# A first stage without loops, mask transposes between its node tiles, small loads from ScalarE's queue, and features stored unscaled

## The reference

```
h   = relu(layernorm(x))
g   = (h * node_weights + node_bias + h) @ W
h0  = layernorm(g) * gamma + beta                # features; also the residual
s1  = h0 @ a1;  s2 = h0 @ a2
att = softmax(where(adj > 0, leaky_relu(s1_i + s2_j), -9e15))
x   = x + elu(att @ h0 + h0)
```

## Time and profile before

| | |
|---|---|
| median of 3 runs | 3704.32 us (3702.21 to 3707.39) |
| profiled execution, time | 3706.8 us |
| its span, first to last instruction | 3705.0 us |
| busy, share of the span | TensorE 93%, VectorE 84%, ScalarE 47%, GpSimd 48% |
| mean granted TensorE clock | 0.965 |
| span of first stage and barrier | up to 203.8 us |
| attention stage of layer 0, first matmul | 212.57 us |
| adding up of its last half ends | about 679.5 us |

### The profile page before, as it was taken

The page is one execution under the profiler, slowest core; times in us unless marked ns, Lnnn a source line. Parts: engine busy times, 40 slices in busy tenths (PEclk is TensorE's granted clock), DMA queues, the critical chain, the costliest instruction groups (busy, mean ns, idle before and its releaser), DMA issues. The chain is left out here.

```text
span 3705.0 us, 59650 instructions
## 1 busy us (share of the span) xinstructions
PE 3456.8 (93%) x21147; PEld 1823.0 (49%) x21147; DVE 3098.7 (84%) x7016; ACT 1736.4 (47%) x3578; POOL 1778.2 (48%) x832
## 2 busy tenths in 40 slices
PE   5679999678999999999999999999997999699999
PEld 4579999542111111111111111111116999699999
DVE  6878888577999999999999999999956776477777
ACT  7821111355666666666666666666662444300100
POOL 2400000113888888888888888888890111000000
PEclk8789999888999999999999999999997999899999
DMA  6522121473001110010001111011003332211220
GB/s 237 199 98 87 52 86 58 149 252 116 24 11 28 28 28 15 19 30 28 28 5 28 28 28 28 7 28 28 5 5 104 115 115 81 115 47 61 84 83 27
DMA packets 80079, 240.72 MB, mean 65 GB/s; under 512 B 13616, under 2 KB 40624, under 8 KB 65584
## 3 DMA queue, kind: packets, MB, share of 16 engines
q1 hardware_dynamic: 79792, 236.92, 18.9%
HBM read 151.80 MB, written 85.07 MB: 64 GB/s over the span
## 5 line engine op out<-in xcount | busy, mean ns | idle before, releaser
L1472 POOL TENSOR_TENSOR a_w<-a_w,keep_mask_t 128x1024 f32<-128x1024 f32 x768 | 1627.4, 2145 | 301.1 <-ACT a_w L1457 301.1
L1457 ACT ACTIVATE a_w<-a_sc_ps 128x512 f32<-128x512 f32 x2048 | 1111.4, 595 | 718.1 <-PE a_sc_ps L1379 716.4
L1412 DVE CUSTOM_DVE_ANT_0 a_mx_ps<-a_mx_ps,a_mbias 128x512 f32<-128x512 f32 x1992 | 1310.5, 718 | 74.0 <-PE a_mx_ps L1341 73.2
L1357 PE MATMUL a_o_ps<-a_w,a_v 128*33 128x512 f32 x4096 | 1081.0, 606 | 6.0 <-POOL a_w L1472 5.8
L868 PE MATMUL g_acc<-g_hv,g_w 128*128 128x129 f32 x8192 | 923.6, 276 | 43.2 <-ACT g_hv L825 32.3
L868 PEld LDWEIGHTS g_acc<-g_hv,g_w 128*128 128x128 f32 x8192 | 922.1, 193 | 44.9 <-DVE g_w L804 44.9
L804 DVE SCALAR_TENSOR_TENSOR g_w<-g_row,keep_s,keep_mask_t 128x1024 f32<-128x1024 f32 x512 | 647.1, 1282 | 201.9 <-PE g_acc L868 185.0
L1379 PE MATMUL a_sc_ps<-a_qs,a_ks 97*128 97x512 f16 x2048 | 621.9, 385 | 0.3
L1425 DVE TENSOR_TENSOR a_w<-a_w,keep_mask_t 128x1024 f32<-128x1024 f32 x256 | 457.7, 1788 | 34.0 <-ACT a_w L1457 28.6
L1341 PEld LDWEIGHTS a_mx_ps<-a_ks,a_qs 32*128 32x128 f16 x1992 | 88.9, 91 | 789.3 <-DVE a_mx L1412 427.9
L1341 PE MATMUL a_mx_ps<-a_ks,a_qs 32*128 32x512 f16 x1992 | 376.6, 385 | 7.5 <-DVEq L1429 7.5
(11 more groups left out here) (237 smaller groups left out, 2237.5 us busy)
## 6 DMA issues: line engine op xcount, KB each, us to landing
h_nodes<-p_h SPq DMA_DIRECT2D x16, 1032.0 KB, 3.9
g_h<-h_nodes SPq DMA_DIRECT2D x16, 1032.0 KB, 7.4
p_adj_in<-in_adj SPq DMA_DIRECT2D x16, 1024.0 KB, 8.3
g_row<-u_rows SPq DMA_DIRECT2D x32, 512.0 KB, 7.3
v<-p_v SPq DMA_DIRECT2D x32, 264.0 KB, 3.0
a_v<-v SPq DMA_DIRECT2D x16, 528.0 KB, 3.6
p_x<-in_x SPq DMA_DIRECT2D x8, 1024.0 KB, 5.0
mask_bias<-p_mbias SPq DMA_DIRECT2D x16, 512.0 KB, 8.9
```

What stands on the lines that cost most here:

```text
L1357: mm = nc.tensor.matmul(o_ps[2 * HD * a:2 * HD * a + HD + 1, c % 2, :], v[u][:, jt, a, :], w[:, g % PB, a, :], start=(jt == 0), stop=(jt = ...
L1412: last = nc.vector.tensor_tensor_reduce(out=mx_ps[:, buf, a, :], in0=mx_ps[:, buf, a, :], in1=mbias[:, t, kc * BANK:(kc + 1) * BANK], scal ...
L1457: nc.scalar.activation(w[:, g % PB, a], sc_ps[:, n % SB], ACT.Exp, scale=SCALE).then_inc(exp_done, 1)
L1472: nc.gpsimd.tensor_tensor(w[:, g % PB], w[:, g % PB], keep["mask_t"][:, jt, c * BANK:(c + 1) * BANK].unsqueeze(1).to_broadcast([P, 2, BANK ...
```

## The change

In words:
- All loops of the first stage are gone; every turn is written out, with constants for addresses and waits.
- The masks of turn b are made in turn b (before: those of b+1). TensorE transposes them behind the third and the fourth node group of the turn; before, both stood at its end. ScalarE's copies move with them. The first masks are no longer made before turn 0, and VectorE splits the bias (`split_nb`) ahead of the first statistics.
- VectorE's turn is now mask, shift, statistics of h, mask, statistics of x, scores.
- The seven small loads (weights, bias, gamma, beta, a) are issued by ScalarE, before by SyncE between its large loads.
- The features are stored as projected, without rstd, gamma and beta, with their two score columns, into the DRAM array v. `norm_h` and `affine` are gone. rstd of all batches stays on chip (`keep["u"]`).
- In the attention stage of layer 0, hv is h times (s2_02 times rstd), one product of which GpSimd forms at the end of the first stage, and its last column is s2_02. ScalarE then scales h by rstd for the residual, a second pass of 16 activations per batch. After the division y = att-sum + h, VectorE multiplies y by gamma and adds 2 beta: two more operations of 128x1024 per half. The finishing steps are now five, behind steps 6, 8, 10, 12 and 14.

The diff, cut to its core:

```diff
+def feature_lines(io, b):
+    return io["v"][bass.ds(b, 1)].rearrange("one g p n -> one (g p n)").rearrange("one (p n) -> p (one n)", p=P)[:, 0:T * (F + 2)]
...
         @block.sync    # first stage
             def turn(b, k):
+                if b > 0:
+                    store_h0(b - 1, 1 - k)
+                sp.wait_ge(m01_ready, 2 * b + 1)
+                if b < B - 1:
+                    load_adj(b + 1, 0)
+                store_mbias(b, 0)
+                sp.wait_ge(m01_ready, 2 * b + 2)
+                if b < B - 1:
+                    load_adj(b + 1, 1)
+                store_mbias(b, 1)
+                if b < B - 3:
+                    sp.wait_ge(x_normed, CH * (b + 2))
+                    load_x(b + 3, 1 - k)
...
         @block.gpsimd
-            nc.gpsimd.tensor_tensor(h1[:], h1[:], gamma[:].unsqueeze(1).to_broadcast([P, T, F]), ALU.mult).then_inc(gamma_done, 1)
+            nc.gpsimd.tensor_tensor(keep["v"][:], keep["s2_02"][:], keep["u"][:], ALU.mult).then_inc(value_scaled, 1)
...
         @block.scalar
-            def norm_h(b, k):
-                for t in range(T):
-                    ins = nc.scalar.activation(scaled(b)[:, t, :], h0[k][:, t, 0:F], ACT.Copy, scale=rstd(b)[:, t:t + 1])
...
                 keep_hT(b, 2)
                 ahead(1)
+                keep_mask(b, 0)
                 keep_h0(b, k, 2)
+                keep_h0(b, k, 3)
                 keep_hT(b, 3)
                 ahead(2)
-                keep_h0(b, k, 3)
-                if not last(b):
-                    keep_mask(b, 0)
+                if b < B - 1:
+                    keep_mask(b, 1)
                 keep_h0(b, k, 4)
                 ahead(3)
                 keep_h0(b, k, 5)
...
     FIN = (6, 8, 10, 12, 14) if residual_elu else (10,)    # attention stage
...
+            def scale_y(n):
+                dve.wait_ge(affine_loaded, 32)
+                dve.wait_ge(drained, n + 1 + 2)
+                nc.vector.tensor_tensor(y[:], y[:], gamma[:].unsqueeze(1).to_broadcast([P, IT, F]), ALU.mult).then_inc(gamma_done, 1)
+
+            def shift_y(n):
+                dve.wait_ge(gamma_done, n + 1)
+                nc.vector.scalar_tensor_tensor(out=y[:], in0=beta[:].unsqueeze(1).to_broadcast([P, IT, F]), scalar=2.0, in1=y[:],
+                                               op0=ALU.mult, op1=ALU.add).then_inc(y_ready, 1)
...
             def scale_h(b, k, loads):
                 for t in range(T):
-                    last = nc.scalar.activation(hv[:, k, t, :], h[:, k, t, :], ACT.Copy, scale=value[:, k, t:t + 1])
+                    last = nc.scalar.activation(hv[:, k, t, 0:width], h[:, k, t, 0:width], ACT.Copy, scale=value[:, k, t:t + 1])
+                if residual_elu:
+                    act.wait_ge(h_scaled, 4 * b + 4)
+                    for t in range(T):
+                        last = nc.scalar.activation(h[:, k, t, 0:F], h[:, k, t, 0:F], ACT.Copy, scale=rstd[:, k, t:t + 1])
+                    last.then_inc(h_normed, 1)
```

More of the change, by code:

```diff
@@ L258, in masks_and_nodes0 @@
         CHAIN_H = 5
-        def batches(eng, turn):
-            turn(0, 0, 0)
-            with eng.Fori(0, B // 2 - 2) as i:
-                turn(2 * i + 1, 1, i)
-                turn(2 * i + 2, 0, i + 1)
-            for b in range(B - 3, B):
-                turn(b, b % 2, b // 2)
-        def last(b):
-            return isinstance(b, int) and b == B - 1
-        def first(b):
-            return isinstance(b, int) and b == 0
-        def late(b):
-            return isinstance(b, int) and b >= B - 2
         def rstd(b):
-            return rstd_last[:] if last(b) else rstd_h[:]
-        def scaled(b):
-            return hn[0] if last(b) else h1
+            return keep["u"][:, b, :]
         @block.sync
@@ L601, in _ @@
                 norm_x(0, 0, q)
-            batches(act, turn)
-            norm_h(B - 1, 1)
+            for b in range(B):
+                turn(b, b % 2)
+            keep_mask(B - 1, 1)
             fs.scalar(nc, act, keep)
-            for a in range(2):
-                keep_mask(B - 1, a)
         @block.tensor
@@ L661, in _ @@
             pe.wait_ge(nb_ready, 1)
-            batches(pe, turn)
+            for b in range(B):
+                turn(b, b % 2)
+            turn_mask(B - 1, 1)
             fs.tensor(nc, pe, keep)
@@ L813, in _ @@
                                 finish_stage(stage, 1, 1, 4 * i - 1, 2 * i, i)
-            for stage in range(STAGES):
+            for stage in range(len(FIN)):
                 finish_stage(stage, 1, 1, 2 * B - 1, B, B // 2)
```

233 lines of the change are left out of this document (103 added, 130 removed).

## The result

The changed kernel takes 3669.94 us (median of 4 runs, 3664.86 to 3675.91), the kernel before 3704.48 beside it (4 runs, 3702.21 to 3707.39). The ratio is 0.9907, with a 95% interval of 0.989 to 0.9924: 34.5 us less by the medians. The forecast was 3666. The profiled execution of the changed kernel is the longest of its four (3675.91, span 3674.1; the other spans are 3663.0, 3667.6 and 3668.7), so its rows stand some 6 us on the long side of the median.

The account below looks back on a forecast made before the run. VectorE's cadence was taken to bound first-stage turns. The first attention matmul 41.0 us earlier and 2.4 more at the attention tail gave -38.6: 3668.2 for the profiled execution, 3666 for the median; range 3654 to 3681.

Parts of the forecast that it names:

- W: Start of the first stage: time when the seven small loads have landed, 17.2 before, forecast 12, bounds 8.5 and 15.2.
- the small ones can pass between them: First stage's beginning: small loads can land between four large loads of 4.2 MB that end at some 12.5.
- Rival 3: First stage's beginning: small loads come hardly sooner, landing at 15.2, since queues share DMA engines; total 3669; chance 0.10.
- The turn: One batch of the first stage: some 20.2 us before, forecast 15.8, with 15.2 and 17 as bounds.
- The wait for the power stays: First-stage turn: VectorE still waits 1.62 for GpSimd's power of 4.50, making its need 13.6 + 1.62 = 15.2.
- The low clock: First-stage turn: TensorE partly at 1.2 GHz behind pauses, adding 0.6 to VectorE's 15.2.
- 371 GB/s when full: First-stage turn: full DMA rate, from 293 GB/s at share 0.79, so 5.26 MB take 14.2 us.
- Three limits within one microsecond: First-stage turn: VectorE 15.2, ScalarE about 14.2 and the DMA engines 14.2 lie close, VectorE's being highest.
- The last power: End of the first stage: GpSimd's power for batch 7 ends at 141.2 after the small loads land; 183.4 before.
- The barrier: Between first and attention stages: 4.44 from last store to next stage's first load, kept in the forecast as 4.4.
- Cost nil: Attention stage: two added VectorE operations per half stay hidden, with 1.7 us of cover, except 2.4 at the end.
- Four periods of 116.3 behind it unchanged: Layer 0's attention, behind the first matmul: its four TensorE rounds keep their length of 116.3 each.

Follow-up runs that it names:

- sp_loads: Changed kernel with the seven small loads back in SyncE's queue, at their places in the kernel before; 3673.28 us, ratio 0.9909.
- dve_more: Changed kernel plus one unread VectorE product (gamma times features, 2.3 us) in each first-stage turn but the first; 3676.32 us, ratio 0.991.
- less_adj: Changed kernel with the second adjacency block of each pair loaded once instead of every turn, 4.2 MB a turn instead of 5.26; median 3669.65 us, ratio 0.9909.
- no_affine: Changed kernel without the two VectorE operations applying gamma and beta in layer 0's attention; 3669.47 us, ratio 0.9903.
- pad32: Changed kernel with 32 unused semaphore increments at the end of TensorE's first-stage code, moving its attention loop; 3665.64 us, ratio 0.9892.
- bpad143: Kernel before the change with 143 unused semaphore increments at the end of TensorE's first-stage code; 3721.70 us, ratio 1.004.
- pad240: Changed kernel with 240 unused semaphore increments at the end of TensorE's first-stage code; 3712.05 us, ratio 1.0018.

## Why the prediction was right, point by point

The time was 4 us above the forecast and well inside the range, but several of its terms missed, and that they nearly cancelled is luck. The first matmul came at 171.85 for a forecast of 171.6, because small loads that landed 3.3 later than forecast met a barrier 2.4 shorter and turns that took 0.7 less in all. The attention stage lost 11.7 that nobody had forecast. Of that 4.5 came back in code that did not change, and another 3.5 because the profiled execution lies 6.0 above its median, where I had taken 2.5.

- **W**, forecast 12, measured 15.34: the failed step is "the small ones can pass between them". Rival 3 is what happened, with its 15.2. The cause of even this small gain was not the queue (sp_loads).
- **The turn**, forecast 15.8, measured 15.6 in the profile (15.33 over four kernels). The size held, the reason did not. "The wait for the power stays" was wrong: the shift waited for nothing in the five turns. The term behind it was the 4.50 of the power, taken from a row with a mask beside it; it measured 2.90 to 3.57. The low clock that I priced at 0.6 is there in three of the five turns, but the turns do not get longer with it. What holds the turn above VectorE's 13.6 is late loads (5.5 us for x and 3.3 for the adjacency over the five turns) and ScalarE's features (4.1). The rate of 371 GB/s when full held, with 369, and with it the 14.2 us for a turn's bytes; yet at a share of 0.93 single loads came up to 2.6 us late. dve_more and less_adj say that no single limit rules: VectorE's 13.6, ScalarE's 14.0, the 14.2 of the bytes and the 13.9 and more of the ring of one buffer lie close together. "Three limits within one microsecond" was the right sentence, "VectorE's the highest" was not.
- **The last power** at W + 141.2 is at W + 140.5 (155.82). The store of the row factors follows 5.4 later (forecast 5.5), with 0.22 for the 16x16 operation that took 3.13. Both sums hold, the first of them with the turn for the wrong reason.
- **The barrier.** I took over the 4.44 from last store to next load; it is 2.03. The last store there was 1 MB of features, a kind that took 4.8 us from issue to landing; now it is the 64 KB of row factors, which take 1.5. From there to the first matmul 8.6 (forecast 8.5). So the 171.6 of the forecast, plus 3.3 for W, less 0.7, 0.1 and 2.4, plus 0.1, is the measured 171.85 but for rounding.
- **The attention stage.** "Cost nil" for the two operations holds (no_affine), and 2.6 at the tail for 2.4. "Four periods of 116.3 behind it unchanged" failed: 11.7 us more, of which the rounds with a gap account for all but the first round's 0.7: they went to the loop's place in the program. No step of the prediction asked where a loop that is not touched would lie once the code ahead of it is written out. pad32, bpad143 and pad240 show this cause from three sides, and the instruction transfers show it at work.
- **The sum.** Two parts remain open. Between the end of layer 0 and the end of the program the kernels of this study need 3019.5 to 3033.3 us for the same code; the highest is pad240's, and layer 3's loop explains 12 of it, but without it the others still lie between 3019.5 and 3029.3, and that is not explained. The 11.1 us that pad32 wins in its stretch are 8.8 in the spans of the two profiled executions, because 0.4 is lost ahead of the stretch and 2.0 behind it, and 5.5 in the medians.

## What to carry to other kernels

Writing out a stage moves every loop behind it. Look in the new trace at the return of each long loop for a few matmuls followed by an "issue" gap, and if there is one, shift the loop by a few dozen cheap instructions at a place where the engine waits anyway. Small loads on which a stage begins should be issued ahead of the megabytes, whichever queue they use. And when a change takes work off one engine, ask for the bytes per turn and for the ring of the most urgent single buffer before counting all of the work as gain.

## What the runs showed of the hardware that was not expected

- At a return to the top of TensorE's loop of 1024 matmuls every kernel here shows 1.6 to 2.2 us of idle time, put down to VectorE's weights although these were there, and, at some places of the loop, a second stall 2 to 13 matmuls later. The later it comes, the shorter it is: 2.3 to 2.5 us behind two matmuls, 1.8 to 2.2 behind five, 1.6 to 1.8 behind eight, 0.9 to 1.2 behind thirteen. A 16 KB instruction transfer that starts 0.3 to 0.4 us behind the first matmul (once 0.7) ends 1.2 to 1.6 us ahead of the end of that stall.
- Such a gap costs nearly as much again in the clock: the three rounds with 1.9 us gaps have 350.4 us of matmuls in the changed kernel, 345.5 in pad32 and in the kernel before, and 344.6 in pad240, behind gaps of 1.0 us.
- A semaphore increment of TensorE takes about 0.14 us: 240 of them spread the store of the row factors and the next stage's first load from 2.0 to 36.3 us. With 32 they ran partly beside the store, and the spread was 4.4.
- With the transfer engines busy 0.93 of the time, x took 9.3 us from issue to landing and an adjacency block 10.8 (medians over the five turns), where it had been 5.1 and 8.2 at a share of 0.69 (92.45 to 153.92 of the kernel before).
